# Moving the second group's operand split, its row maxima and two chunk loads in the cross-attention of a fused two-layer decoder

## The reference, cut to what matters

```python
q = _qdq(x) @ _qdq(wq).T + bq
kv = cond @ wkv.T + bkv
k, v = jnp.split(kv, 2, axis=-1)
# q, k, v as (B, N or M, H, Dh)
attn = jax.nn.softmax(jnp.einsum('bnhd,bmhd->bhnm', q, k) * scale, axis=-1)
o = jnp.einsum('bhnm,bmhd->bnhd', attn, v).reshape(B, N, C)
out = _qdq(o) @ _qdq(wp).T + bp
```

## Time and profile before

| what | before |
|---|---|
| median of three runs | 1986.0 us (1974.71 to 2152.21) |
| the profiled execution's own time | 1987.1 us |
| its span, first to last instruction | 1985.2 us |
| outside the span | 1.9 us |
| TensorE busy, share of the span | 94% |
| granted clock of TensorE, mean | 0.977 |

### The profile page before, as it was taken

One profiled execution on the slowest core, in us unless ns is written; L12 is line 12 of the kernel. 1 busy time (PEld: TensorE's weight loads), 2 busy tenths in 40 slices (PEclk: granted clock), 3 DMA queues, 4 the chain that ended last, 5 costly groups with the idle time before them and its releaser, 6 DMA issues. The chain is left out here.

```text
span 1985.2 us, 25443 instructions
## 1 busy us (share of the span) xinstructions
PE 1875.4 (94%) x9812; PEld 1428.0 (72%) x9816; DVE 1247.6 (63%) x2196; ACT 664.1 (33%) x1054; POOL 225.3 (11%) x192
## 2 busy tenths in 40 slices
PE   7899988999999999989999999999989999999997
PEld 5677877444443588958888888888878775788885
DVE  5423745565771655576787787787762489765665
ACT  3312231345445355423342342333234331221211
POOL 0000101121110000010121121111210001212212
PEclk9899998799999899999999999999999999999999
DMA  5101220322330300032122223313212110111001
GB/s 213 43 0 62 93 69 11 81 63 69 71 93 22 106 1 1 1 105 96 60 100 96 85 71 105 109 38 130 75 34 74 64 39 5 64 43 43 22 1 43
DMA packets 67191, 124.16 MB, mean 63 GB/s; under 512 B 8576, under 2 KB 27008, under 8 KB 65536
## 3 DMA queue, kind: packets, MB, share of 16 engines
q1 hardware_dynamic: 67072, 122.53, 19.6%
HBM read 88.82 MB, written 14.68 MB: 52 GB/s over the span
## 5 line engine op out<-in xcount | busy, mean ns | idle before, releaser
L780 DVE TENSOR_REDUCE b_nm<-ps 128x1 f32<-128x1024 f32 x128 | 153.6, 1220 | 92.2 <-PE ps L768 92.2
L1260 ACT ACTIVATE b_pr<-ps 128x512 f32<-128x512 f32 x256 | 133.2, 604 | 138.4 <-PE ps L1174 138.4
L229 PE MATMUL ps<-d_x_high,d_w_high 128*128 128x512 f32 x384 | 154.3, 402 | 1.7 <-issue 1.7
L231 PE MATMUL ps<-d_x_high,d_w_low 128*128 128x512 f32 x384 | 149.8, 390 | 0.0
L230 PE MATMUL ps<-d_x_low,d_w_high 128*128 128x512 f32 x384 | 149.7, 390 | 0.0
L1186 PE MATMUL ps<-b_pr,b_VS 128*64 128x512 f32 x512 | 126.6, 617 | 0.0
L768 PE MATMUL ps<-b_kS,b_qS 96*128 96x512 f32 x256 | 86.6, 423 | 12.8 <-DMA b_qS<-b_q_parts 10.6
L2163 POOL TENSOR_TENSOR d_sqsum<-d_sqsum,d_sq 128x512 f32<-128x512 f32 x32 | 45.4, 1422 | 468.3 <-ACT d_sq L2074 468.1
L1174 PEld LDWEIGHTS ps<-b_qS,b_kS 98*128 98x128 f32 x256 | 44.0, 193 | 74.0 <-issue 50.9
L1174 PE MATMUL ps<-b_qS,b_kS 98*128 98x512 f32 x256 | 92.9, 444 | 4.5 <-ACT b_pr L1260 2.6
L229 PEld LDWEIGHTS ps<-d_x_high,d_w_high 128*128 128x128 f32 x384 | 72.2, 188 | 17.3 <-issue 2.1
(11 more groups left out here) (429 smaller groups left out, 4843.9 us busy)
## 6 DMA issues: line engine op xcount, KB each, us to landing
b_kS<-b_k_parts SPq DMA_DIRECT2D x96, 128.0 KB, 2.3
f_rows<-d_fw SPq DMA_DIRECT2D x24, 512.0 KB, 3.5
f_w<-f_rows SPq DMA_DIRECT2D x12, 1024.0 KB, 4.8
b_qS<-b_q_parts SPq DMA_DIRECT2D x96, 64.0 KB, 2.0
a_convT<-in_convT SPq DMA_DIRECT2D x4, 1024.0 KB, 13.1
d_w<-in_d_wq SPq DMA_DIRECT2D x16, 256.0 KB, 3.8
d_w<-in_d_wk SPq DMA_DIRECT2D x16, 256.0 KB, 2.9
d_w<-in_d_wg SPq DMA_DIRECT2D x16, 256.0 KB, 3.6
```

Source lines behind the costliest of these rows:

```text
L229: nc.tensor.matmul(out, lhsT[0], rhs[0], start=start, stop=False)
L231: return nc.tensor.matmul(out, lhsT[1], rhs[0], start=False, stop=stop)
L780: nc.vector.tensor_reduce(nm[:, g % 2, u:u + 1], c.ps[:, banks:banks + 2, :], AX.XY, ALU.max, negate=True).then_inc(job_read, 1)
L1260: nc.scalar.activation(pr[:, n % RING, :], c.ps[:, 4 + n % BANKS, :], ACT.Exp).then_inc(exp_done, 1)
```

## The change

1. GpSimd splits group 1 in the first block (`split_group` moves ahead of the blocks, and its four parts for group 1 stand behind `root_pool` there). In the second block GpSimd goes from `values(0)` to `values(1)` and the split of group 2.
2. Group 1's maxima stand in slots 3 to 12 and not in 0 to 9: `first_slot(1, u)` is 3 + 10u // 16, that is two in slots 3, 4, 6, 8, 9 and 11 and one in 5, 7, 10 and 12. Its turn stands in slot 13 and not in 11. All other groups keep their slots.
3. On SyncE, `context(6)` stands ahead of all waits for the split of group 0, and `context(7)` stands between the transfers of heads 1 and 2.

```diff
+    def first_slot(g, u):
+        return SLOTS * (g - 1) - LEAD + u if g > 1 else 3 + 10 * u // UNITS
+
     for slot in range(2 * NSS + 5):
         g, here = slot // SLOTS, len(JOBS)
-        JOBS += [("max", gg, u) for gg in range(1, NG) for u in range(UNITS) if max(0, SLOTS * (gg - 1) - LEAD + u) == slot]
+        JOBS += [("max", gg, u) for gg in range(1, NG) for u in range(UNITS) if first_slot(gg, u) == slot]
...
-        if g + 1 < NG and slot % SLOTS == TURN_AT:
+        if g + 1 < NG and slot % SLOTS == (TURN_AT if g else 13):
             JOBS.append(("turn", g + 1, 0))
...
             context(4)
             context(5)
+            context(6)
             sp.wait_ge(split_done, 2)
             sp.wait_ge(split_low, 2)
             sp.wait_ge(q_ready, QJOBS)
             sp.wait_ge(turned, len(SOURCES))
             for h in range(4):
                 split_rows(sp, 0, h)
-            context(6)
-            context(7)
+                if h == 1:
+                    context(7)
             maxima_rows(sp, 0)
...
             first_norm.root_pool(pool, slice(TT - 1, TT))
+            for part in range(4):
+                split_group(pool, 1, part)
...
             values(0)
-            for part in range(4):
-                split_group(1, part)
             for g in range(NG):
                 values(2 * g + 1)
                 if g + 2 < NG:
                     for part in range(4):
-                        split_group(g + 2, part)
+                        split_group(pool, g + 2, part)
```

More of the change, by code:

```diff
@@ L793, in turn_maxima_dve, with split_group @@
         nc.vector.memset(mark[:], 0.0).then_inc(job_read, 1)
+    def split_group(pool, g, part):
+        b, f = GROUPS[g]
+        k, q = KF[:, f, b * KEYS:(b + 1) * KEYS], qF[:, f, b * BANK:(b + 1) * BANK]
+        if part == 0:
+            for h in range(4):
+                pool.wait_ge(in_st[(g - 1) % 2][h], 96 * ((g - 1) // 2 + 1))
+        src, parts = ((k, k_parts), (q, q_parts))[part % 2]
+        if part < 2:
+            nc.gpsimd.tensor_copy(parts[:, 0, :], src).then_inc(split_done, 1)
+        else:
+            pool.wait_ge(split_done, 2 + 4 * (g - 1) + part - 1)
+            nc.gpsimd.tensor_tensor(parts[:, 1, :], src, parts[:, 0, :].bitcast(F32), ALU.subtract).then_inc(split_done, 1)
     QJOBS = 2 * KD
@@ L1049, in _ @@
         def _(pool):
[L1050 to L1062, removed]
             def values(q):
```

## The result

| what | before | after |
|---|---|---|
| median | 1985.67 us (12 runs) | 1973.24 us (12 runs, 1968.55 to 1975.56) |
| ratio of the times | 1 | 0.9942, 95% interval 0.9929 to 0.9954 |
| profiled execution's span | 1985.2 us | 1967.4 us |
| clock granted, mean | 0.977 | 0.986 |

The changed kernel is 12.4 us faster by the medians, 0.6%. The pair of profiled executions is 17.8 us apart, more than the medians; the rows further down say where the rest lies.

A forecast was written before the change was run, and what follows sets the result against it. TensorE, busy 94% of the span, was taken as the bound, with two high waits in cross-attention. 6.4 + 8.3 - 1.0 = 13.7 us off the profiled 1987.1 gave 1973.4; the median, 1.1 lower, 1972.3; range 1959 to 1983.

The forecast's parts named there:

- rival (a): Second block: half clock until 20 us behind the barrier or falling again in a short wait; total gain 10, 1976; chance 0.2.
- the 9 us left to VectorE there: Slots 10 and 11: VectorE, with six maxima and two other jobs, takes no longer than 9 us.
- Chunk loads, 6.4 us: First block, keys of chunk 5: earlier loads save 3.9 us of waiting and 2.5 of half clock.
- GpSimd's split for nothing: First block: group 1's split, 5.15 us, is hidden ahead of the barrier and costs VectorE and TensorE nothing.
- First rows at 6.0 us behind the barrier, a wait of 1.8 left: Slot 3: group 1's first head is ready 6.0 us behind the barrier; 1.8 us of a 10.6 us wait remains.
- The wait of 2.8 us at slot 10: Slot 10: TensorE waits 2.8 us for group 2's first rows, ready 28.2 us behind the barrier.
- The range of the clock, about t0 + 2 to t0 + 12,: Second block: clock at half from about 2 to 12 us behind the barrier's opening, a loss of 1 us.
- the third wait of 1.9 us: Slot 16: the later turn's small transfers land 46.3 us behind the barrier, TensorE is there at 44.4; wait 1.9 us.
- the clock with VectorE's pace: Second block: half clock early on, with VectorE's pace disturbed, loses 1 us, between nothing and 4.8.
- (b): Second block: half clock through all of group 0's supersteps; kernel 6 us slower, 1992; chance 0.05.
- (c): First block: chunk loads do not do what is meant; 6.4 gone, 7.3 left, 1979; chance 0.05.
- (d): Waits at slots 3, 10 and 16 do not arise, transfers landing sooner or TensorE's clock never falling; 16.5 us, 1969; chance 0.15.

The follow-up runs named there:

- e1: Only the chunk loads of the change, added to the kernel before: 1977.29 us, 0.9964 of the kernel before.
- e6: The changed kernel plus matmuls of the identity, results unread, in the second block's first four half steps: 1968.37 us, 0.9922 of the kernel before.
- e10: The changed kernel with group 1's maxima in their old slots but the turn kept in slot 13: 1968.36 us, 0.9937 of the kernel before.
- e2: The changed kernel without the chunk loads, so early split and new slots only: 1981.53 us, 0.9977 of the kernel before.
- e3: The changed kernel with group 1's old slots and the turn in slot 11: 1965.66 us, 0.9905 of the kernel before.
- e5: The changed kernel with group 1's maxima in slots 3 to 10 and the turn in slot 11: 1964.56 us, 0.9912 of the kernel before.
- e8: e5 plus the same unread matmuls as in e6, in the first four half steps: 1967.27 us, 0.9917 of the kernel before.
- e9: e5 with half as many unread matmuls as e8 in the first four half steps: 1963.62 us, 0.9906 of the kernel before.
- e12: The changed kernel with group 1's maxima in slots 4 to 10 and the turn in slot 11: 1970.05 us, 0.9933 of the kernel before.
- e11: The changed kernel run again unaltered, on another chip: 1969.86 us, 0.9934 of the kernel before.
- e4: The changed kernel with the new slots alone, without early split and chunk loads: 1983.00 us, 0.9996 of the kernel before.
- e7: The changed kernel plus ten unread matmuls of the identity ahead of slot 16: 1973.51 us, 0.9947 of the kernel before.

## Why the prediction was right

The time, 1973.2 against 1972.3 forecast, came out by the steps that were named, but the gain of the second block was put at nearly twice what the traces show, and the close agreement is partly luck. Two signs that the prediction itself had named as showing it wrong came: the clock fell again in a short wait, as in rival (a), and slots 10 and 11 took longer than the 9 us left to VectorE there. In the traces the touched part gives 10.3 us, 3.9 of them in the block: that is rival (a)'s sum (10, with 3.5 to 4), and not the forecast's 13.7.

- **Chunk loads, 6.4 us:** 6.4 in the trace, 7.1 (4.2 to 9.9) by e1.
- **GpSimd's split for nothing:** right. It ran from 292.5 to 297.7, VectorE's reductions beside it kept their length, and the first block has the same length with it (changed kernel) and without it (e1): 45.9 us.
- **First rows at 6.0 us behind the barrier, a wait of 1.8 left:** 6.0, and 1.34, since the scores ahead of it ended at 4.7 and not at 4.2.
- **The wait of 2.8 us at slot 10:** it did not come, as TensorE reached slot 10 at 28.4 and not at 24.4; its origin is right (transfers from 22.6 us on), and in e6 0.64 us of it shows. **The range of the clock, about t0 + 2 to t0 + 12,** was 2.5 to 12.7.
- **Slots 12 and 13** took 5.7 us (5.7 to 5.8 forecast), and **the third wait of 1.9 us** was 1.58. e10 shows that the later turn makes it.
- **The term that was mis-sized** is the clock with VectorE's pace, put at 1.0 us. Slots 10 and 11 took 9.5 us where some 7.5 were summed once the rows were there. Of the 2.0 more, 0.9 is VectorE's pace, as e2 takes 8.4 at full clock, and 1.1 the second fall of the clock. The sum had counted six maxima there; the kernel has five, so their pace was undercounted by more than it seems. Behind the third wait half clock cost another 1.6, which the sum ended too early to see: I compared at slot 16 and took both kernels as equal from there. The block gave 3.9 us and not 7.3, 1.9 of the difference ahead of slot 16 (49.2 us behind the barrier against 47.3 forecast) and the rest behind it.
- The touched part is then worth 10.3 us, not 13.7. The medians say 12.4 and 13.4. The other 2 to 3 us lie in stretches that the change does not touch. The profiled pair shows such differences at the same instructions: 2.5 us ahead of the first maximum, and 7.5 in all, with the clock lower in the kernel before in the four windows named above. That makes it likely that they come from where the clock falls, but it was not isolated; why the medians keep some of it stays open. The forecast of slot 16 at 379, against 379.50, was luck in the same way: the barrier opened 2.5 us early, and the slot lay 2.9 us later behind it than summed without the clock's term.
- **The part of the change I took for a gain and that is a loss** is the spreading of the maxima past slot 11. I costed it step by step within one sum and never summed the early split with the old slots. e3 shows 7.7 us for that at slot 22, against 3.9 with the new slots and the later turn. The later turn alone is 3.1 of that (e10), and maxima spread over slots 3 to 10 cost nothing (e5, slot 22 at 60.3 against e3's 60.8).

Rivals (b) and (c) did not occur. Of (d) only the wait at slot 10 stayed out, and not because transfers landed sooner.

## What to carry to other kernels

A schedule that starts work sooner is only summed up when its last deadline is looked at too: here the maxima were spread past slot 11, the turn had to follow them, and its transfers then came late for the next group. When a change has parts, sum each part alone before trusting the whole; the one that looks like the finishing touch may be the one that costs. And where a low-clock stretch lies ahead of a fixed arrival, as of group 2's rows at slot 10, it is free up to the arrival (e6); the one behind the last wait was paid in full (1.6 us at slot 16). Last, a single trace carries its own falls of the clock: a gain of 2 or 3 us at one point of it is not yet a gain in the median (e8, e9, e12).

## What the runs showed of the hardware

- A wait of 1.57 to 1.68 us of TensorE at slot 16, among full work, was followed by half clock in the next superstep in five kernels: the changed one, e2, e6, e10 and e11 (5.5 or 5.6 us in place of 3.94). In e4, where the same wait is 1.58 us, the superstep behind it took its normal 3.9 us (slot 16 at 52.5, slot 18 at 56.5). A wait of this length can bring the clock down and need not.
- Matmuls that do nothing but fill a wait kept the clock at 1.00 through that wait in all four kernels that had them. In e9's trace this was worth 2.9 us of 60 at slot 22; the medians do not show it. Each of them in 32-bit floats runs as two instructions, about 0.11 us each at full clock (20 in 2.25 us in e7), so a count from the source fills twice what it seems to.
